# Expert products of a routed feed-forward layer: each 128-row matmul issued as two 64-row tiles with their own PSUM banks

## The chip, the cores and the metric

The kernel runs on one core of a Trainium2 chip. What is measured is the device time of one execution in microseconds (us). TensorE (PE in the profile; its weight loads are PEld) multiplies, VectorE (DVE) and ScalarE (ACT) work on tiles in SBUF and PSUM, GpSimd (POOL) issues the gathers and scatters by index, SyncE (SP) issues most other transfers. PSUM has 8 banks; a bank holds 512 float32 per partition.

## The reference, cut to what matters

```python
def conv(x, w, b):                       # depthwise, causal: 8 taps per channel
    return conv_general_dilated(x, w, (1,), padding=[(7, 0)], feature_group_count=1024) + b

def ffn(y, w_router, w_experts):         # top-1 routing over 8 experts
    idx = argmax(einsum('bsh,eh->bse', y, w_router), -1)
    all_out = einsum('bsh,efh->bsef', y, w_experts)
    return take_along_axis(all_out, idx[:, :, None, None], axis=2)[:, :, 0, :]

out = x + ffn(conv(x, cond), w_router, w_experts)   # x: 8 x 512 x 1024, experts: 8 x 1024 x 1024, float32
```

## The kernel before

There are 4096 tokens of 1024 channels. The kernel has two stages.

Stage one is the convolution. It is done on TensorE as matmuls of 128 columns (line 807, `conv`), 512 of them in four groups of two batches; each float32 matmul appears in the trace as two. ScalarE copies the results out of six PSUM banks (0 to 5, lines 435 and 436, semaphore `conv_out`). VectorE picks each token's expert (`choose`), TensorE counts places with a few bfloat16 matmuls (`rank`, banks 6 and 7), VectorE turns the places into row numbers (`place_rows`, semaphore `pos_ready`), and GpSimd scatters the convolved rows to DRAM, sorted by expert.

Stage two is the expert product. The sorted rows are taken in slots of 128 tokens of one expert: 35 slots with these inputs. For slot t:

- VectorE turns the loaded block so that channels lie on partitions (`turn_blocks`, line 683, into `y_cols`); ScalarE rounds it to the one-pass float32 type (`high_y`, line 449, `ys` HI) and VectorE subtracts to get the rest (`low_y`, line 688, `ys` LO, semaphore `ys_lo`).
- The expert's weights lie in SBUF split in the same way (`w_sb` HI and LO; ScalarE line 444, VectorE line 674 in `low_w`, semaphore `w_split`). They are replaced chunk by chunk, only when the expert changes.
- TensorE's `gemm(t, k, nth)` (line 836) makes 8 chunks of 128 channels x 3 products (HI·HI, HI·LO, LO·HI) x 2 halves of 512 output columns: 48 matmuls, all from line 851. The slot's sums lie in one of two pairs of banks, `out_banks = [4, 0]`, that is banks 4, 5 for even slots and 0, 1 for odd ones. In the last chunk the three products of the left half come first (semaphore `half_out`), then those of the right half (`gemm_chunk`).
- VectorE's `residual(t)` adds each half of the sums to the gathered row of x (lines 696 and 698); GpSimd then scatters the row to the output (line 930) and, when that has landed, gathers the x row of slot t + 2 into the same buffer (line 923).

The order of the work on each engine is written out by hand. On VectorE the loop body for slot t is `turn_blocks(t + 1)`, `residual(t - 1)`, `low_y(t + 1)`, `low_w(t + 1)`, so `low_y(t + 1)`, for which `gemm(t + 1)` waits, stands behind `residual(t - 1)`. `gemm(t)` waits for `ys_lo`, for `res_done` of slot t - 2 (its banks), and every second chunk for `w_split`. Inside `gemm(0)`, behind its third chunk, stands the last group's `rank`. Slots 0 to 2 stand ahead of a loop, the rest are in it, two to a round.

Of the kernel before, what the change touches and what calls it, by code (L numbers as in the profile page):

```python
# [6 lines left out]
ALU = mybir.AluOpType  # L7
# [9 lines left out]
BATCH, SEQ, H, TAPS, EXPERTS = 8, 512, 1024, 8, 8  # L17
TOKENS = BATCH * SEQ
HC = H // P
GROUP = 2  # L20
GROUPS = BATCH // GROUP
GT = GROUP * SEQ
TPG = GT // P
TILES = TOKENS // P
HALF = 512
# [4 lines left out]
HI, LO = 0, 1  # L30
# [10 lines left out]
SIDE = PHASES * CH  # L41
# [7 lines left out]
BANKS = -(-SETS // PER_BANK)  # L49
# [5 lines left out]
def bank_sets(n):  # L55
    return range(n * PER_BANK, min((n + 1) * PER_BANK, SETS))
# [17 lines left out]
LAST = GROUPS - 1  # L74
# [90 lines left out]
def build(nc, x_both, x_t, x_rows, factors_t, experts, consts, out):  # L165
    ctx = ExitStack()
    with ctx:  # L167
        def sb(name, shape, dt=F32):
            return ctx.enter_context(nc.sbuf_tensor(name, shape, dt))

        def over(name, shape, at, dt=F32):
            return nc.alloc_sbuf_tensor_at(name, shape, dt, offset=at)

        def sem(name):
            return ctx.enter_context(nc.semaphore(name))
# [5 lines left out]
        w_sb = sb("w_sb", [P, HC, 2, H], F32R)  # L181
# [15 lines left out]
        x_row = over("x_row", [P, RING, H], raw_at + 24 * KB)  # L197
        cmp = over("cmp", [P, 3, SLOTS, EXPERTS], x_at)
        assert 32 * KB <= row_bytes
        ys = [over("ys0", [P, 2, HC, P], raw_at, F32R), over("ys1", [P, 2, HC, P], x_at + 8 * KB, F32R)]  # L200
# [28 lines left out]
            return cst[:, at:at + n]  # L229

        ps = ctx.enter_context(nc.psum_tensor("ps", [P, 8, HALF], F32))
        out_banks = [4, 0]
        out_ps = [ps[:, b:b + 2, :].rearrange("p a n -> p (a n)") for b in out_banks]

        def conv_bank(n):
            return ps[:, n % CONV_BANKS, :]

        def rank_ps(g):
            return ps[:, 6 + g % 2, 0:(TPG + 1) * EXPERTS].rearrange("p (t e) -> p t e", t=TPG + 1)

        const_in = sem("const_in")
        factors_in = [sem(f"factors_in{k}") for k in range(len(FACTOR_PACKS))]
# [9 lines left out]
        conv_out = sem("conv_out")  # L252
# [5 lines left out]
        pos_ready = sem("pos_ready")  # L258
# [15 lines left out]
        ys_lo = sem("ys_lo")  # L274
        gemm_chunk = sem("gemm_chunk")
        half_out = sem("half_out")
        res_done = sem("res_done")
        row_out = [sem(f"row_out{k}") for k in range(RING)]

# [215 lines left out]
        def _(dve):  # L495
            V = nc.vector
# [69 lines left out]
            count, lead, others, rest, start, n_of, flag, more, nth, tmp, tail, done, sign = (per[:, i, :] for i in range(1, 14))  # L566
# [124 lines left out]

            def residual(t, k, nth_of_ring):

                dve.wait_ge(half_out, t + 1)
                dve.wait_ge(x_got[k], nth_of_ring * 16)  # L695
                V.tensor_tensor(x_row[:, k, 0:HALF], out_ps[k][:, 0:HALF], x_row[:, k, 0:HALF], ALU.add)  # L696
                dve.wait_ge(gemm_chunk, (t + 1) * HC)
                V.tensor_tensor(x_row[:, k, HALF:], out_ps[k][:, HALF:], x_row[:, k, HALF:], ALU.add).then_inc(res_done, 1)  # L698

            def low_w(t):  # L700
                new = dve.value_load(tab_i[0:1, 2, bass.ds(t, 1)], min_val=0, max_val=2)  # L701
# [17 lines left out]
            for g in range(1, GROUPS):  # L719
                n = g * PACKS  # L720
# [40 lines left out]
            slot_starts()  # L761
            low_y(2, 0)
            residual(0, 0, 1)
            slot_table()
            turn_blocks(FIRST, FIRST % RING, FIRST // RING + 1)
# [6 lines left out]
            with dve.Fori(0, ROUNDS) as i:  # L772
                with dve.If(i < last + 1):
                    for k in range(RING):
                        t = i * RING + (FIRST + k)
# [8 lines left out]
        @block.tensor  # L784
        def _(pe):
            def conv(g, s):
                n, b = g * PACKS + s // PACK, s // PER_BANK
                if s % PACK == 0:
                    if n == 0:
                        pe.wait_ge(mats_ready, 1)  # L790
                        pe.wait_ge(x_start, 16)
                    elif g == 0:
                        pe.wait_ge(mats_ready, n + 2)
                        pe.wait_ge(x_in[n % X_RING], (n // X_RING + 1) * 16)
                    else:
                        pe.wait_ge(doubled, n - PACKS + 1)
                if g == 0 and s == START_SETS:
                    pe.wait_ge(mats_ready, 2)
                    pe.wait_ge(x_in[0], 16)
                sets = bank_sets(b)  # L800
                bank = g * BANKS + b
                if s == sets[0] and bank >= CONV_BANKS:

                    pe.wait_ge(conv_out, bank - CONV_BANKS + 1)
                k = s - sets[0]
                to = conv_bank(bank).rearrange("p (u n) -> p u n", n=SIDE)[:, k:PER_BANK + 1:PER_BANK - k, :]
                mm = nc.tensor.matmul(to, xs[:, n % X_RING, s % PACK, :], mats[:, s, :].rearrange("p (u n) -> p u n", n=SIDE),  # L807
                                      start=(s == sets[0]), stop=(s == sets[-1]), skip_group_check=True)
                if s + 1 in ENDS:
                    mm.then_inc(conv_mm, 1)  # L810

            def rank(g):

                pe.wait_ge(chosen_ready, g + 1)
                pe.wait_ge(const_in, 16)
                if g >= 2:

                    pe.wait_ge(pos_ready, g - 1)
                nc.tensor.matmul(rank_ps(g)[:, 0:TPG, :], before[:, 0:P], chosen[:, :, :], start=True, stop=False,
                                 skip_group_check=True)  # L820
                for t in range(TPG):
                    mm = nc.tensor.matmul(rank_ps(g)[:, t + 1:, :], before[:, P:],
                                          chosen[:, t, :].unsqueeze(1).to_broadcast([P, TPG - t, EXPERTS]),
                                          start=False, stop=(t == TPG - 1), skip_group_check=True)
                mm.then_inc(ranked, 1)

            pe.wait_ge(warm_zero, 1)
            for n in range(START_MATMULS):
                nc.tensor.matmul(ps[:, 7, 0:P], zeros[:, :], zeros[:, :], start=True, stop=True, skip_group_check=True)
            for g in range(GROUPS):  # L830
                for s in range(SETS):
                    if g and s == 3 * PACK:
                        rank(g - 1)
                    conv(g, s)

            def gemm(t, k, nth):

                pe.wait_ge(ys_lo, t + 1)
                if not (isinstance(t, int) and t < RING):

                    pe.wait_ge(res_done, t - 1)
                for c in range(HC):
                    if nth is None:

                        pe.wait_ge(w_split, c + 1)
                    elif c % 2 == 0 and nth is not True:

                        pe.wait_ge(w_split, nth * HC + (c + 2))

                    def product(a, b, f):  # L850
                        return nc.tensor.matmul(out_ps[k][:, f * HALF:(f + 1) * HALF], ys[k][:, a, c, :],  # L851
                                                w_sb[:, c, b, f * HALF:(f + 1) * HALF],
                                                start=(c == 0 and (a, b) == (HI, HI)),
                                                stop=(c == HC - 1 and (a, b) == (LO, HI)))

                    if c < HC - 1:
                        for a, b in PRODUCTS:
                            for f in range(2):
                                mm = product(a, b, f)
                    else:  # L860
                        for a, b in PRODUCTS:
                            mm = product(a, b, 0)
                        mm.then_inc(half_out, 1)
                        for a, b in PRODUCTS:
                            mm = product(a, b, 1)
                    mm.then_inc(gemm_chunk, 1)
                    if nth is None and c == 2:
                        rank(LAST)

            def load_of(t):  # L870
                return pe.value_load(tab_i[0:1, 1, bass.ds(t, 1)], min_val=0, max_val=EXPERTS - 1)

            pe.wait_ge(conv_out, GROUPS * BANKS - 4)
            gemm(0, 0, None)
            pe.wait_ge(conv_out, GROUPS * BANKS)
            gemm(1, 1, True)
            gemm(2, 0, True)
            pe.wait_ge(table_ready, 1)
            last = pe.value_load(one_i[0:1, 3:4], min_val=0, max_val=ROUNDS - 1)
            full = pe.value_load(one_i[0:1, 5:6], min_val=0, max_val=ROUNDS)  # L880
            with pe.Fori(0, ROUNDS) as i:
                with pe.If(i < last + 1):
                    gemm(i * RING + FIRST, FIRST % RING, load_of(i * RING + FIRST))
                    with pe.If(i < full):
                        gemm(i * RING + (FIRST + 1), (FIRST + 1) % RING, load_of(i * RING + (FIRST + 1)))
# [133 lines left out]
```

## Time and profile before

| | |
|---|---|
| time, median of 2 runs | 522.23 us (520.93 and 523.53) |
| the profiled execution: its own time | 518.85 us |
| the profiled execution: span, first to last instruction | 517.0 us |
| PE busy | 503.7 us, 97% of the span |
| PEld busy | 435.7 us, 84% |
| DVE busy | 287.8 us, 56% |
| ACT busy, POOL busy | 150.5 us, 134.0 us |
| matmuls of line 851 | 1680, which is 35 slots x 48 |

A row of the profile names line, engine, operation and tile (written tile first, then the read ones), shapes, a count, busy time and the mean duration of one. The matmuls overlap in their pipeline, so their mean duration (389 ns for line 851) is longer than the time from one to the next; that time is read from a count in a stretch. Times in a timeline are from the start of the span.

### The profile page before, as it was taken

To read this page: it belongs to the slowest core of one execution; us is meant where nothing else is said; L and a number is where in the kernel's file an instruction comes from. 1 tells how busy PE (TensorE), PEld (TensorE's weight loads), DVE (VectorE), ACT (ScalarE), POOL (GpSimd) and SP (SyncE) were. 2 spreads that over 40 slices of the span, in tenths; PEclk is the share of its full clock that TensorE was granted. 3 is DMA by queue.
4 is the path that set the end of the run, shared out by engine and by line. 5 is a ranking of instruction groups with operands and counts; after the bars stand their busy time and mean duration, and the time that the engine had idled before them with its cause. 6 is when DMAs were issued, how large, how long until landed. Compare 5 with 4: busy or idle time off the path is not lost.

```text
span 517.0 us, 9479 instructions
## 1 busy us (share of the span) xinstructions
PE 503.7 (97%) x2764; PEld 435.7 (84%) x2765; DVE 287.8 (56%) x418; ACT 150.5 (29%) x255; POOL 134.0 (26%) x148
## 2 busy tenths in 40 slices
PE   8999999998997999999999999999999999999995
PEld 8999999997886877888888888888888888888884
DVE  5947373769965034499773432664347244482961
ACT  2444444376001010166530100521034011340710
POOL 0003224170650112332322321213212222222312
PEclk9999999999999999999999999999999999999999
DMA  8976999997579998689999565496658855535445
GB/s 294 411 207 211 406 283 403 335 357 262 191 301 278 318 411 219 203 275 356 377 346 305 167 196 169 134 373 188 179 180 316 255 147 151 170 105 158 130 146 171
DMA packets 59623, 130.31 MB, mean 252 GB/s; under 512 B 12752, under 2 KB 32720, under 8 KB 59600
## 3 DMA queue, kind: packets, MB, share of 16 engines
q1 hardware_dynamic: 41696, 70.12, 43.7%
q0 software_dynamic: 14832, 54.27, 29.3%
q10 hardware_dynamic: 3072, 5.65, 3.4%
q8 instruction: 10, 0.16, 0.1%
q14 instruction: 13, 0.11, 0.1%
HBM read 94.56 MB, written 35.45 MB: 251 GB/s over the span
## 4 chain that ended last, share of the span: by engine, by line
PE 63%; issue 2%; DMA 2%; DVE 0%; DVEq 0%; POOL 0%; POOLq 0%
PE ps L851 63%; DMA x_row<-x_rows,idx 2%; DVE ys L688 0%; DMA out<-x_row,idx 0%; POOL out L930 0%; DVEq L167 0%; DVEq L701 0%; DVE x_row L698 0%; POOL idx L937 0%; DVE x_row L696 0%; DVEq L703 0%; POOLq L971 0%; DVEq L695 0%; POOLq L929 0%; POOLq L922 0%
## 5 line engine op out<-in xcount | busy, mean ns | idle before, releaser
L851 PE MATMUL ps<-w_sb,ys 128*128 128x512 f32 x1680 | 382.2, 389 | 4.2 <-DVE ys L688 3.7
L851 PEld LDWEIGHTS ps<-w_sb,ys 128*128 128x128 f32 x1680 | 314.9, 188 | 70.9 <-issue 5.1
L683 DVE STREAM_TRANSPOSE y_cols<-y_blk 128x1024 f32<-128x1024 f32 x36 | 44.8, 1244 | 147.8 <-PE ps L851 122.7
L807 PE MATMUL ps<-mats,xs 128*128 128x128 f32 x1024 | 118.3, 279 | 1.2 <-DMA xs<-x_both 1.2
L807 PEld LDWEIGHTS ps<-mats,xs 128*128 128x128 f32 x1024 | 117.3, 195 | 1.7 <-DVE mats L506 1.4
L449 ACT CAST ys<-y_cols 128x1024 fp32r<-128x1024 f32 x36 | 37.9, 1053 | 275.5 <-DVE y_cols L683 267.1
L674 DVE TENSOR_TENSOR w_sb<-w_raw,w_sb 128x1024 fp32r<-128x1024 f32 x56 | 64.2, 1220 | 3.3 <-ACT w_sb L444 3.3
L930 POOL DMA_INDIRECT out<-x_row,idx x35 | 41.1, 1175 | 83.9 <-DVE x_row L698 79.9
L937 POOL COPY idx<-ids_all 128x1 int32 (+1 forms) x36 | 15.0, 416 | 178.2 <-DMA out<-x_row,idx 115.8
L444 ACT CAST w_sb<-w_raw 128x1024 fp32r<-128x1024 f32 x56 | 56.5, 1052 | 9.4 <-PE ps L851 8.3
L918 POOL DMA_INDIRECT y_sorted<-rows,pos_i x32 | 37.0, 1157 | 75.3 <-PE ps L807 55.8
L514 DVE COPY xs<-xs 56x1008 f32<-56x1008 f32 x48 | 33.2, 691 | 24.6 <-DMA xs<-x_t 22.7
L923 POOL DMA_INDIRECT x_row<-x_rows,idx x36 | 38.5, 1070 | 31.0 <-POOL idx L937 30.1
L688 DVE TENSOR_TENSOR ys<-y_cols,ys 128x1024 fp32r<-128x1024 f32 x36 | 44.0, 1223 | 0.5 <-ACT ys L449 0.5
L435 ACT COPY part<-ps 128x64 f32<-128x64 f32 x76 | 22.0, 289 | 66.6 <-PE ps L807 54.0
L436 ACT COPY rows<-ps 128x448 f32<-128x448 f32 (+1 forms) x76 | 40.8, 540 | 0.0
L696 DVE TENSOR_TENSOR x_row<-ps,x_row 128x512 f32<-128x512 f32 x35 | 23.2, 664 | 26.4 <-DMA x_row<-x_rows,idx 19.6
L698 DVE TENSOR_TENSOR x_row<-ps,x_row 128x512 f32<-128x512 f32 x35 | 23.7, 676 | 0.0
L504 DVE TENSOR_TENSOR mats<-factors 128x512 f32<-128x512 f32 (+1 forms) x17 | 11.2, 658 | 5.4 <-DMA factors<-factors_t 5.4
L506 DVE TENSOR_TENSOR mats<-factors 128x512 f32<-128x512 f32 (+1 forms) x17 | 11.2, 656 | 0.0
L674 DVE TENSOR_TENSOR w_sb<-w_first,w_sb 128x1024 fp32r<-128x1024 f32 x8 | 9.7, 1222 | 1.0 <-ACT w_sb L444 0.9
L444 ACT CAST w_sb<-w_first 128x1024 fp32r<-128x1024 f32 x8 | 8.5, 1066 | 0.0
(102 smaller groups left out, 47.1 us busy)
## 6 DMA issues: line engine op xcount, KB each, us to landing
w_raw<-experts SPq DMA_DIRECT2D x56, 512.0 KB, 8.2
y_blk<-y_sorted SPq DMA_DIRECT2D x152, 128.0 KB
xs<-x_both SPq DMA_DIRECT2D x15, 512.0 KB
xs<-x_t SPq DMA_DIRECT2D x28, 256.0 KB
xs<-x_t ACTq DMA_DIRECT2D x20, 256.0 KB
w_first<-experts SPq DMA_DIRECT2D x8, 512.0 KB, 10.2
ids_all<-y_sorted SPq DMA_DIRECT2D x38, 1.0 KB
x_row<-x_rows,idx POOLq DMA_INDIRECT x36
```

Of the source, the lines that this page charges most:

```text
L436: nc.scalar.copy(to, conv_bank(n)[:, 0:m * SIDE].rearrange("p (c j i) -> p j c i", j=PHASES, i=CH)).then_inc(conv_out, 1)
L444: nc.scalar.copy(w_sb[:, c, HI, :], raw[:, c, :]).then_inc(w_hi, 1)
L449: nc.scalar.copy(ys[k][:, HI, :, :].rearrange("p c s -> p (c s)"), y_cols[k][:, :, :].rearrange("p c s -> p (c s)")).then_inc(ys_hi, 1)
L514: V.tensor_copy(xs[old:old + USED, s, :, :].rearrange("p c (b t) -> p (c b) t", b=GROUP)[:, :, 1:], xs[new:new + USED, s, :, :].rearrange( ...
L674: V.tensor_tensor(w_sb[:, c, LO, :], raw[:, c, :], w_sb[:, c, HI, :].bitcast(F32), ALU.subtract).then_inc(w_split, 1)
L683: V.transpose(y_cols[k][:, :, :].rearrange("p m (t i) -> p t m i", t=4), y_blk[k][:, :, :, :]).then_inc(y_blocks, 1)
L688: V.tensor_tensor(ys[k][:, LO, :, :].rearrange("p c s -> p (c s)"), y_cols[k][:, :, :].rearrange("p c s -> p (c s)"), ys[k][:, HI, :, :].r ...
L807: mm = nc.tensor.matmul(to, xs[:, n % X_RING, s % PACK, :], mats[:, s, :].rearrange("p (u n) -> p u n", n=SIDE), start=(s == sets[0]), sto ...
L851: return nc.tensor.matmul(out_ps[k][:, f * HALF:(f + 1) * HALF], ys[k][:, a, c, :], w_sb[:, c, b, f * HALF:(f + 1) * HALF], start=(c == 0 ...
L918: G.indirect_dma_start(y_sorted, at(pos_i[:, g, j:j + 1]), rows[g % 2][:, j, :], None, bounds_check=last_row, oob_is_err=False).then_inc(y ...
L923: G.indirect_dma_start(x_row[:, k, :], None, x_rows, at(index), bounds_check=last_token, oob_is_err=False).then_inc(x_got[k], 16)
L930: G.indirect_dma_start(out, at(index), x_row[:, k, :], None, bounds_check=last_token, oob_is_err=False).then_inc(row_out[k], 16)
```

## The change

Each of the 48 matmuls of a slot has 128 rows (input channels) of weights and data. The change issues it as two matmuls of 64 rows, rows 0 to 63 and rows 64 to 127, each in its own row tile of TensorE's array (`tile_position` (0, 0) and (64, 0); `SIDE` is 64). Each row tile sums into its own pair of banks: banks 4, 5 and 6, 7 for even slots, 0, 1 and 2, 3 for odd ones. VectorE adds both sums to the row of x: four adds where there were two, with a semaphore `res_part` between the two that write the same half. Because a slot now holds four banks, the last group's `rank` moves to bank 0, waits there until all convolution banks are copied out, and `gemm(1)`, which writes bank 0, waits for `place_rows` of the last group.

```diff
-        out_banks = [4, 0]
-        out_ps = [ps[:, b:b + 2, :].rearrange("p a n -> p (a n)") for b in out_banks]
+        out_banks = [(4, 6), (0, 2)]
+        out_ps = [[ps[:, b:b + 2, :].rearrange("p a n -> p (a n)") for b in banks] for banks in out_banks]
...
-            return ps[:, 6 + g % 2, 0:(TPG + 1) * EXPERTS].rearrange("p (t e) -> p t e", t=TPG + 1)
+            return ps[:, 6 + g % 2 if g < LAST else 0, 0:(TPG + 1) * EXPERTS].rearrange("p (t e) -> p t e", t=TPG + 1)
...
+                left, right = slice(0, HALF), slice(HALF, H)
                 dve.wait_ge(half_out, t + 1)
                 dve.wait_ge(x_got[k], nth_of_ring * 16)
-                V.tensor_tensor(x_row[:, k, 0:HALF], out_ps[k][:, 0:HALF], x_row[:, k, 0:HALF], ALU.add)
+                V.tensor_tensor(x_row[:, k, left], out_ps[k][0][:, left], x_row[:, k, left], ALU.add).then_inc(res_part, 1)
+                dve.wait_ge(res_part, 2 * t + 1)
+                V.tensor_tensor(x_row[:, k, left], out_ps[k][1][:, left], x_row[:, k, left], ALU.add)
                 dve.wait_ge(gemm_chunk, (t + 1) * HC)
-                V.tensor_tensor(x_row[:, k, HALF:], out_ps[k][:, HALF:], x_row[:, k, HALF:], ALU.add).then_inc(res_done, 1)
+                V.tensor_tensor(x_row[:, k, right], out_ps[k][0][:, right], x_row[:, k, right], ALU.add).then_inc(res_part, 1)
+                dve.wait_ge(res_part, 2 * t + 2)
+                V.tensor_tensor(x_row[:, k, right], out_ps[k][1][:, right], x_row[:, k, right], ALU.add).then_inc(res_done, 1)
...
-                if g >= 2:
+                if g == LAST:
+                    pe.wait_ge(conv_out, GROUPS * BANKS)
+                elif g >= 2:
...
-                        return nc.tensor.matmul(out_ps[k][:, f * HALF:(f + 1) * HALF], ys[k][:, a, c, :],
-                                                w_sb[:, c, b, f * HALF:(f + 1) * HALF],
-                                                start=(c == 0 and (a, b) == (HI, HI)),
-                                                stop=(c == HC - 1 and (a, b) == (LO, HI)))
+                        for s in range(2):
+                            rows_of = slice(s * SIDE, (s + 1) * SIDE)
+                            mm = nc.tensor.matmul(out_ps[k][s][:, f * HALF:(f + 1) * HALF], ys[k][rows_of, a, c, :],
+                                                  w_sb[rows_of, c, b, f * HALF:(f + 1) * HALF],
+                                                  start=(c == 0 and (a, b) == (HI, HI)),
+                                                  stop=(c == HC - 1 and (a, b) == (LO, HI)),
+                                                  tile_position=(s * SIDE, 0))
+                        return mm
...
             pe.wait_ge(conv_out, GROUPS * BANKS - 4)
+            pe.wait_ge(pos_ready, LAST)
             gemm(0, 0, None)
-            pe.wait_ge(conv_out, GROUPS * BANKS)
+            pe.wait_ge(pos_ready, GROUPS)
             gemm(1, 1, True)
```

On VectorE, in the body of the loop, one slot's work from the turned block to the rest of `ys` stands like this before (`y_cols_53` is the block's turned tile, `ys_57` the slot's split tile, ISA and REGISTER_ALU are steps of the sequencer):

```order
283 L683 STREAM_TRANSPOSE y_cols_53<-y_blk 128x4x8x32 [waits gemm_chunk]
284 L695 ISA [waits half_out]
285 L696 TENSOR_TENSOR x_row<-ps,x_row 128x512 [waits x_got0]
286 L698 TENSOR_TENSOR x_row<-ps,x_row 128x512 [waits gemm_chunk]
287 L687 REGISTER_ALU
288 L688 TENSOR_TENSOR ys_57<-y_cols_53,ys_57 128x1024 [waits ys_hi]
```

and like this with the change:

```order
287 L684 STREAM_TRANSPOSE y_cols_53<-y_blk 128x4x8x32 [waits gemm_chunk]
288 L697 ISA [waits half_out]
289 L698 TENSOR_TENSOR x_row<-ps,x_row 128x512 [waits x_got0]
290 L699 ISA
291 L700 TENSOR_TENSOR x_row<-ps,x_row 128x512 [waits res_part]
292 L702 TENSOR_TENSOR x_row<-ps,x_row 128x512 [waits gemm_chunk]
293 L703 REGISTER_ALU
294 L704 TENSOR_TENSOR x_row<-ps,x_row 128x512 [waits res_part]
295 L688 REGISTER_ALU
296 L689 TENSOR_TENSOR ys_57<-y_cols_53,ys_57 128x1024 [waits ys_hi]
```

Two adds with waits for the add just ahead of them have come between the turned block and the subtraction that gives `ys` LO; nothing else moved.

On TensorE, the slots 1 and 2 and the start of the loop stand like this with the change (`ys_58` is the split tile of odd slots, `ys_57` that of even ones):

```order
346 L861 MATMUL ps<-w_sb,ys_58 128x512 [waits ys_lo,pos_ready]
347 L861 MATMUL ps<-w_sb,ys_58 128x512 x95
348 L861 MATMUL ps<-w_sb,ys_57 128x512 [waits res_done,ys_lo]
349 L861 MATMUL ps<-w_sb,ys_57 128x512 x95
350 L892 TENSOR_LOAD one_i [waits table_ready]
```

A slot is 96 matmuls in place of 48, each still with 512 columns, and the first of slot 1 waits for `pos_ready`, where the kernel before waited for `conv_out`.

## Rows read from the trace of the kernel before

**Rows 1.** The page: busy time, and granted TensorE clock in 40 slices
```profile
PE 503.7 (97%) x2764; PEld 435.7 (84%) x2765; DVE 287.8 (56%) x418; ACT 150.5 (29%) x255; POOL 134.0 (26%) x148
PEclk9999999999999999999999999999999999999999
```

**Rows 2.** Chain that ended last, in time order: start us, us, what
```profile
184.55 11.17 PE ps L851 x48
195.72 0.15 issue
195.87 315.14 PE ps L851 x1389
```

**Rows 3.** Windows, line 851 alone: stretch, us, busy (instructions), clock, DMA, GB/s
```profile
260.00:380.00 120.00, 120.00 (x531) 99.38 (x530) 1.00 0.70 225
```

**Rows 4.** Windows, line 807 alone (convolution, 128 columns)
```profile
20.00:40.00 20.00, 20.00 (x181) 20.00 (x180) 1.00 0.81 264
40.00:60.00 20.00, 19.93 (x179) 19.76 (x178) 1.00 0.82 298
```

**Rows 5.** Groups by line: busy us, mean ns | idle before
```profile
L851 PE MATMUL ps<-w_sb,ys 128*128 128x512 f32 x1680 | 382.2, 389 | 4.2 <-DVE ys L688 3.7 <-ACT rows L436 0.4 <-issue 0.2
L851 PEld LDWEIGHTS ps<-w_sb,ys 128*128 128x128 f32 x1680 | 314.9, 188 | 70.9 <-issue 5.1 <-ACT rows L436 0.5
L807 PEld LDWEIGHTS ps<-mats,xs 128*128 128x128 f32 x1024 | 117.3, 195 | 1.7 <-DVE mats L506 1.4 <-issue 0.2
```

**Rows 6.** Timeline of DVE, choosing: start us, us, engine, line
```profile
127.91 0.23 DVE L544 TENSOR_TENSOR logits<-logits,most 128x64 f32<-128x64 f32 x1
128.17 0.22 DVE L545 TENSOR_REDUCE top<-logits 128x8 f32<-128x64 f32 x1
```

**Rows 7.** Timeline of DVE ahead of slot 3
```profile
158.85 0.65 DVE L696 TENSOR_TENSOR x_row<-ps,x_row 128x512 f32<-128x512 f32 x1
159.42 0.67 DVE L698 TENSOR_TENSOR x_row<-ps,x_row 128x512 f32<-128x512 f32 x1
160.03 1.23 DVE L688 TENSOR_TENSOR ys<-y_cols,ys 128x1024 fp32r<-128x1024 f32 x1
```

**Rows 8.** Timeline of DVE ahead of slot 5
```profile
181.90 0.69 DVE L696 TENSOR_TENSOR x_row<-ps,x_row 128x512 f32<-128x512 f32 x1 [1.64 <-DMA x_row<-x_rows,idx]
182.51 0.68 DVE L698 TENSOR_TENSOR x_row<-ps,x_row 128x512 f32<-128x512 f32 x1
183.10 1.22 DVE L688 TENSOR_TENSOR ys<-y_cols,ys 128x1024 fp32r<-128x1024 f32 x1
```

**Rows 9.** Timeline of PE from slot 0 on, [idle before <- releaser]
```profile
129.94 28.81 PE L851 MATMUL ps<-w_sb,ys 128*128 128x512 f32 x126
...
161.49 22.07 PE L851 MATMUL ps<-w_sb,ys 128*128 128x512 f32 x96 [2.75 <-DVE ys L688]
184.55 11.17 PE L851 MATMUL ps<-w_sb,ys 128*128 128x512 f32 x48 [0.99 <-DVE ys L688]
```

**Rows 10.** Timeline of DVE, placing the last group
```profile
132.59 0.17 DVE L563 CAST pos_i<-pos 128x8 int32<-128x8 f32 x1
```

**Rows 11.** Timeline of all engines at the end
```profile
499.73 11.95 PE L851 MATMUL ps<-w_sb,ys 128*128 128x512 f32 x52
511.14 0.69 DVE L696 TENSOR_TENSOR x_row<-ps,x_row 128x512 f32<-128x512 f32 x1 [6.72 <-PE ps L851]
511.75 0.68 DVE L698 TENSOR_TENSOR x_row<-ps,x_row 128x512 f32<-128x512 f32 x1
513.26 1.01 POOL L930 DMA_INDIRECT out<-x_row,idx  x1 [1.48 <-DVE x_row L698]
```

**Rows 12.** Lines 848, 884 and 851: durations min/median/max ns, first and last start us
```profile
L848 PEldq FUSED_REGOPS  x32: 42/42/47, 161.4 to 497.7; - x32
L848 PEldq ALU_OP  x96: 32/32/32, 161.7 to 504.7; - x96
L884 PEldq COMPARE_BRANCH  x16: 71/71/73, 168.5 to 496.6; - x16
L851 PE MATMUL ps<-w_sb,ys x1680: 387/389/494, 123.8 to 511.3; 128*128 128x512 f32 x187
```

More of the change, by code:

```diff
@@ L276, in build @@
         half_out = sem("half_out")
+        res_part = sem("res_part")
         res_done = sem("res_done")
```

## The prediction

> **What bounds the kernel now.** I read the page's busy times first: TensorE is busy for 503.7 of 517.0 us, and its granted clock is full (2.4 GHz) in all 40 slices [rows 1]. So the time is TensorE's, and only its pace and its few stops count. Next the chain of waits, in order of time: from 195.87 us on it is one piece of 315.14 us with 1389 matmuls of line 851, and no other engine stands in it until the last slot is done [rows 2]. The pace is 315.14 / 1389 = 0.2269 us per matmul; a window in the middle of it says 120 / 531 = 0.2260 us [rows 3], and I use 226.9 ns. At 2.4 GHz 512 columns take 512 / 2.4 = 213.3 ns, so 13.6 ns of each are something other than streaming columns: 1680 x 13.6 ns = 22.8 us in all. That is everything the change could win on the products.
>
> The stops of line 851 add up to 4.2 us, of which 3.7 us are waits for VectorE's line 688, `low_y` [rows 5]: ahead of slot 3 (2.75 us) and of slot 5 (0.99 us) [rows 9]. VectorE's share of 56% hides that these two stops hang on it.
>
> **The change: TensorE.** A product is now two loads and two matmuls, and a slot has 96 of each. The columns per matmul stay 512. If the two row tiles run at the same time, a product still takes one stream of 512 columns in each; if they don't, it takes two in turn. No row of before shows row tiles, so I bound this from both sides.
>
> - Loads. The convolution shows the closest thing to twice the loads: each of its matmuls has its own load of 128 columns of four bytes, and 179 of them pass in 20 us, which is 111.7 ns for a load with its matmul [rows 4]; the two kinds of load are alike, 188 and 195 ns in mean [rows 5]. Two of them are 223.5 ns, 3.4 ns less than a product takes now. So neither the loads nor the sequencer, which issued those pairs at that rate, should hold two tiles back, though only just.
> - Matmuls, lower end: the 13.6 ns vanish, because one tile streams while the other changes its weights: 213.3 ns per product, -22.8 us. The 111.7 ns pace gives 223.5 ns and -5.7 us.
> - Matmuls, upper end: tiles in turn, 453.8 ns per product, +381 us.
> - I take the middle: each tile's own stream keeps the 226.9 ns that a stream takes now, since nothing in a tile's stream has changed but the number of rows, and the other tile lies beside it. Change: 0.
>
> In the trace the load of the next weights lies beside the running matmul on the same 128 rows: a load with its own turn would make the pace at least 111.7 + 213.3 = 325 ns, and it is 226.9 [rows 2, 4]. The Trainium skill (TensorE: Matmul & The Clock Gate, Part 3: Packing small matmuls, The mechanism) says that a load overlaps a running matmul only where the row group differs. For a full-height stream this trace does not agree, which is why I don't count a gain from loads that could only now be hidden. The same section's table gives 3.07 times for four row tiles, 77% of the ideal; a product at 226.9 / 0.77 = 295 ns would by that estimate add 114 us. No run here shows it yet.
>
> **The change: VectorE.** `residual` goes from two adds to four. Adds that don't depend on each other start 0.57 to 0.61 us apart (158.85, 159.42, then line 688 at 160.03) and last 0.65 to 0.69 us [rows 7, 8]. One that waits for the one ahead of it starts 0.03 us behind its end: line 544 at 127.91 lasts 0.23 us, line 545 starts at 128.17 [rows 6]. So four adds occupy 0.68 + 0.6 + 0.68 + 0.6 = about 2.6 us where two took 1.2: +1.4 us per slot, 35 x 1.4 = 49 us of VectorE, which then is busy for 337 of some 520 us. In most slots this costs nothing, since TensorE works 48 x 0.2269 = 10.9 us on a slot and has no stop after 195.87 us [rows 2]. It counts in three places, where what it delays is already waited for:
>
> - Slot 3: `low_y(3)` stands behind `residual(1)` and TensorE waits for it (160.03 + 1.23 = 161.26, matmul at 161.49) [rows 7, 9]: +1.4 us.
> - Slot 5: `residual(3)` starts when the gather of its row of x lands, and `low_y(5)` ends at 184.32, the matmul starts at 184.55 [rows 8, 9]. The gather hangs, by the scatter, on `residual(1)`, so it moves by the same 1.4 us as TensorE did; the longer `residual(3)` then adds its own +1.4 us.
> - The end: the left half is free at 511.14, the right half added by 511.75 + 0.68 = 512.43, then the last scatter is issued [rows 11]. With four adds this ends 1.4 us later: +1.4 us.
>
> Together +4.2 us. If these waits lost their cover in every slot, the bound is 35 x 1.4 = 49 us; if later gathers absorb the delay, it is only the end's 1.4 us.
>
> **The change: banks, waits, sequencer.** `gemm(1)` now waits for the last `place_rows`. That ends at 132.59 + 0.17 = 132.76 us; `gemm(1)` starts 30 matmuls after 129.94, at 136.75 [rows 9, 10]: 4 us of cover, cost nothing. `rank` moved to bank 0 waits for copies that end before TensorE gets there. The sequencer runs ahead of the array: its last wait for weights (chunk 6 of the last slot) is at 504.7 us, the last matmul starts at 511.3, so chunk 6 starts at 511.3 - 11 x 0.227 = 508.8: 4.1 us or 18 matmuls ahead. From the branch of line 884 (496.6) to the first weights' wait of the next slot (497.7) it needs 1.1 us [rows 12]. With half the columns per instruction of work, 18 matmuls are 9 products, 2.0 us: still covered.
>
> **Sum.** 518.85 us (the profiled execution, 517.0 of it the span) + 0 + 4.2 = 523.05, so **523 us**. The profiled run lies 3.4 us under the median of the two runs shown, 522.23, so I read the result as about 1% slower, within the 2% that a measurement of this kernel can tell from no change.
>
> **Rivals.**
>
> 1. *The gap between matmuls vanishes* (the side of faster). 13.6 ns per product are hidden by the other tile: 523 - 22.8 = 500 us; from 218 ns per product down, it is over 2% faster. For: a row's own gap could lie under the other tile's stream. Against: loads are hidden already, and the loads' pace of 223.5 ns lies above 218.
> 2. *The gap comes twice* or the sequencer's run-ahead fails. If the 13.6 ns belong to each change of weights and the tiles share it, a product takes 240.5 ns: +22.8, 546 us. It decides from 231 ns on. If the 1.1 us of each slot's branch come to light in 32 slots: +35, 558 us. For: two loads of 111.7 ns leave only 3.4 ns, and 2.0 us of run-ahead is only twice what a branch needs.
> 3. *A tile's load waits for its own matmul.* Each tile then takes 111.7 + 226.9 = 338.6 ns per product, both tiles side by side: 523 + 1680 x 111.7 ns = 711 us. This is what the Trainium skill's rule above would give. Against: the overlap on the same rows in the trace of before. Anything halfway between one and two streams falls here too.
> 4. *The tiles don't run together.* 453.8 ns per product: 523 + 381 = 904 us. The change then does not do what it says. For: no row shows two matmuls in the array. Against: the two tiles share neither rows nor banks.
>
> **How the numbers follow.** Forecast (224 to 231 ns a product; 514 to 529 us) 0.47; rival 1, 0.15; rival 2, 0.18; rival 3, 0.08; rival 4, 0.12. Faster by over 2%: 0.15. Within 2%: 0.47. Slower: 0.18 + 0.08 + 0.12 = 0.38. The range reaches from rival 1 to the far end of rival 2, 500 to 558 us, and leaves out rivals 3 and 4, 0.20. The likeliest case alone has 514 to 529.
>
> **What would show it.** In the profile after: 3360 matmuls of line 861 with the count per stretch doubled (1062 in 120 us) for the forecast, 1130 for rival 1, near 530 for rival 4, near 710 for rival 3. The four adds should take 2.6 us from first start to `low_y`; the stops ahead of slots 3 and 5 should be about 1.4 us longer each, and the last add should end 2.7 us after its first began. A stop at each slot's first matmul with nothing that it waits for would be the sequencer. The forecast is wrong if the pace of a product leaves 224 to 231 ns; VectorE alone can't move it by 2%.

## The result, and the profile after

The changed kernel takes 531.14 us (median of 529.4 and 532.89) where the kernel before takes 522.23: a ratio of 1.0189, 95% interval 1.0128 to 1.025. Beside other kernels on a second chip it came out at 531.32 against 520.4 us, ratio 1.0168 (1.0106 to 1.023). The ratios here and below are estimates from the runs of both kernels, each with its interval; the plain quotients of the medians differ a little (1.0171 and 1.0210). So it is slower by 1 to 2.5%. The forecast was 523 us, about 1% slower, in a range of 500 to 558.

The profiled execution took 532.89 us with a span of 530.7 us, 13.7 us more than the span before. It is the longer of the two executions shown, and the profiled one of the kernel before (518.85 us) is the shortest of three, so the two traces differ by more than the medians do (8.9 us). Its page begins (busy us, share, count; then the granted clock in 40 slices):

```profile
PE 508.5 (96%) x4444; PEld 465.8 (88%) x4445; DVE 334.9 (63%) x488; ACT 150.2 (28%) x255; POOL 133.5 (25%) x148
...
PEclk9999999999899989999999899999999999999998
```

Against [rows 1]: 1680 more matmuls and loads, 47 us more of VectorE, only 4.8 us more of TensorE, and a clock that is no longer full everywhere. Line 861 alone, in a stretch without stops (stretch, us, busy and count of PE and PEld, clock):

```profile
300.00:420.00 120.00, 120.00 (x1062) 109.75 (x1061) 1.00 0.66 213
```

1062 matmuls are 531 products in 120 us, exactly the count of [rows 3]: a product of two tiles keeps the pace of one full-height matmul. So the loss lies elsewhere. The timeline of TensorE, whose last bracket is the idle time before a piece and what ended it:

```profile
131.07 0.24 PE L827 MATMUL ps<-chosen,cst 128*128 128x64 bf16 x1 [2.66 <-DVE chosen L551]
...
131.50 31.54 PE L861 MATMUL ps<-w_sb,ys 64*128 64x512 f32 x252
163.44 22.08 PE L861 MATMUL ps<-w_sb,ys 64*128 64x512 f32 x192 [0.40 <-DVE ys L689]
188.61 67.19 PE L861 MATMUL ps<-w_sb,ys 64*128 64x512 f32 x576 [3.09 <-DVE ys L689]
256.54 22.06 PE L861 MATMUL ps<-w_sb,ys 64*128 64x512 f32 x192 [0.74 <-DVE ys L689]
279.37 11.18 PE L861 MATMUL ps<-w_sb,ys 64*128 64x512 f32 x96 [0.77 <-DVE ys L689]
293.53 230.39 PE L861 MATMUL ps<-w_sb,ys 64*128 64x512 f32 x2016 [2.98 <-DVE ys L689]
```

Where [rows 9] had two stops on `low_y`, there are five, 8.0 us in sum, and three of them (256.54, 279.37, 293.53) stand where TensorE had none before [rows 2]. The first matmul after the last `rank` starts 1.56 us later than before (131.50 for 129.94), that of slot 3 1.95 us, that of slot 5 4.06 us; the last matmul starts at 523.5 for 511.3 [rows 12], 12.2 us later. Nothing shows the 1.56 us to be the change's: ahead of the last `choose` VectorE waited 1.74 us for the transfer of a block, where it had waited 0.46, and nothing that the change touches stands before that. In the variants below that do all the work the same start lies between 129.78 and 131.77 us.

What stands behind the last and longest of the new stops is in the chain of waits, in order of time (start us, us, what):

```profile
267.95 10.04 DMA out<-x_row,idx
278.28 0.92 POOL idx L950
...
280.04 9.36 DMA x_row<-x_rows,idx
289.43 0.70 DVE x_row L698
...
292.24 1.07 DVE ys L689
293.53 229.73 PE ps L861 x2007
```

A slot's row of x is gathered into the buffer from which another slot's result is scattered: the scatter (10.04 us) must land, then the index is copied, the gather (9.36 us) lands, and only then can `residual` begin, with `low_y` behind it. The expert weights load at the same time: eight loads of 512 KB are issued from 265.89 us on, and they land after 9.6 us (median).

The scatters of slots 10 and 12, which share a buffer, give the length of a round of this loop (timeline of GpSimd, here and then in the kernel before):

```profile
267.95 1.93 POOL L943 DMA_INDIRECT out<-x_row,idx  x1 [0.30 <-issue]
293.22 1.01 POOL L943 DMA_INDIRECT out<-x_row,idx  x1 [0.30 <-issue]
...
258.83 1.93 POOL L930 DMA_INDIRECT out<-x_row,idx  x1 [0.30 <-issue]
282.22 1.01 POOL L930 DMA_INDIRECT out<-x_row,idx  x1 [0.30 <-issue]
```

From one to the next are 25.3 us, 23.4 in the kernel before, and TensorE needs only 2 x 10.9 = 21.8 us for two slots. So even before the change the loop was slower than TensorE in this stretch, but TensorE did not yet have to wait there.

The second part of the loss is the clock. Windows over all engines (stretch, us, busy and count of PE, PEld, DVE, ACT, POOL, then clock, DMA, GB/s):

```profile
124.00:132.00 8.00, 5.30 (x47) 4.86 (x49) 6.02 (x12) 2.04 (x3) 0.00 (x0) 0.90 0.39 107
132.00:165.00 33.00, 32.60 (x266) 27.72 (x264) 25.82 (x70) 2.10 (x2) 15.65 (x16) 0.92 0.75 256
165.00:190.00 25.00, 21.91 (x188) 20.11 (x186) 10.68 (x13) 2.21 (x3) 3.94 (x6) 0.97 1.04 339
190.00:195.00 5.00, 5.00 (x38) 4.14 (x36) 0.00 (x0) 0.94 (x1) 0.61 (x1) 0.81 1.03 404
...
260.00:295.00 35.00, 31.26 (x272) 26.54 (x270) 24.07 (x26) 10.60 (x11) 9.43 (x9) 0.99 0.85 260
295.00:300.00 5.00, 5.00 (x36) 4.13 (x34) 3.70 (x5) 0.53 (x1) 0.83 (x2) 0.73 0.76 251
```

After three stops (2.66, 3.09 and 2.98 us) the clock stood at its lower level, 1.2 GHz, for a while. With only two levels, a mean of 0.92 over 33 us is 33 x 0.08 x 2 = 5.3 us at the lower one; the six rows together give 1.6 + 5.3 + 1.5 + 1.9 + 0.7 + 2.7 = 13.7 us. At that level a product takes nearly twice as long (427 ns, seen with one tile alone in an experiment below), so the estimate is a cost of about 13.7 x (1 - 227/427) = 6.4 us, a little less as the first fall began within the stop. The pieces agree: the 252 matmuls from 131.50 us on take 31.54 us, where a variant below with a full clock took 28.86. Part of that cost is not a loss: what the clock took between 131 and 163 us shortened the stop ahead of slot 3 from 2.75 to 0.40 us.

The end is as forecast (timeline, all engines):

```profile
523.39 0.69 DVE L698 TENSOR_TENSOR x_row<-ps,x_row 128x512 f32<-128x512 f32 x1 [5.30 <-PE ps L861]
524.12 0.69 DVE L700 TENSOR_TENSOR x_row<-ps,x_row 128x512 f32<-128x512 f32 x1
524.72 0.68 DVE L702 TENSOR_TENSOR x_row<-ps,x_row 128x512 f32<-128x512 f32 x1
525.44 0.69 DVE L704 TENSOR_TENSOR x_row<-ps,x_row 128x512 f32<-128x512 f32 x1
```

526.13 - 523.39 = 2.74 us where [rows 11] show 512.43 - 511.14 = 1.29: 1.45 us more.

### The profile page after: what moved, and what is told of

Same layout as the page of the kernel before. It is cut to its first block, busy times and chain, and to the rows that moved or that the text cites. A ratio compares the mean times of both kernels' runs of the same rounds, so it can differ in the third digit from the quotient of the medians.

```text
span 530.7 us, 12976 instructions
## 1 busy us (share of the span) xinstructions
PE 508.5 (96%) x4444; PEld 465.8 (88%) x4445; DVE 334.9 (63%) x488; ACT 150.2 (28%) x255; POOL 133.5 (25%) x148
## 4 chain that ended last, share of the span: by engine, by line
PE 50%; DMA 7%; issue 5%; DVE 4%; ACT 1%; POOL 1%; DVEq 1%; ACTq 0%; POOLq 0%
PE ps L861 50%; DMA x_row<-x_rows,idx 4%; DMA out<-x_row,idx 4%; DVE w_sb L675 1%; ACT w_sb L445 1%; DVE x_row L702 1%; DVE x_row L698 1%; DVE y_cols L684 0%; POOL idx L950 0%; DVE ys L689 0%; DVEq L707 0%; DVE x_row L704 0%; POOL out L943 0%; DVEq L710 0%; ACTq L458 0%
## 5 line engine op out<-in xcount | busy, mean ns | idle before, releaser
L861 PE MATMUL ps<-w_sb,ys 64*128 64x512 f32 x3360 | 388.8, 391 | 8.5 <-DVE ys L689 8.0
L861 PEld LDWEIGHTS ps<-w_sb,ys 64*128 64x128 f32 x3360 | 347.2, 187 | 49.5 <-issue 10.1
L813 PE MATMUL ps<-mats,xs 128*128 128x128 f32 x1024 | 116.3, 276 | 3.3 <-DMA xs<-x_both 1.6
L813 PEld LDWEIGHTS ps<-mats,xs 128*128 128x128 f32 x1024 | 115.0, 192 | 4.1 <-DVE mats L507 2.3
L950 POOL COPY idx<-ids_all 128x1 int32 (+1 forms) x36 | 16.6, 462 | 171.3 <-DMA out<-x_row,idx 142.0
L931 POOL DMA_INDIRECT y_sorted<-rows,pos_i x32 | 35.2, 1101 | 73.5 <-PE ps L813 54.1
L515 DVE COPY xs<-xs 56x1008 f32<-56x1008 f32 x48 | 33.3, 694 | 24.8 <-DMA xs<-x_t 23.4
L698 DVE TENSOR_TENSOR x_row<-ps,x_row 128x512 f32<-128x512 f32 x35 | 23.2, 663 | 30.1 <-DMA x_row<-x_rows,idx 24.8
L700 DVE TENSOR_TENSOR x_row<-ps,x_row 128x512 f32<-128x512 f32 x35 | 24.2, 691 | 1.2
L704 DVE TENSOR_TENSOR x_row<-ps,x_row 128x512 f32<-128x512 f32 x35 | 24.2, 691 | 1.2
L702 DVE TENSOR_TENSOR x_row<-ps,x_row 128x512 f32<-128x512 f32 x35 | 23.8, 680 | 0.0
```

The costliest lines, as they stand in the source:

```text
L515: V.tensor_copy(xs[old:old + USED, s, :, :].rearrange("p c (b t) -> p (c b) t", b=GROUP)[:, :, 1:], xs[new:new + USED, s, :, :].rearrange( ...
L861: mm = nc.tensor.matmul(out_ps[k][s][:, f * HALF:(f + 1) * HALF], ys[k][rows_of, a, c, :], w_sb[rows_of, c, b, f * HALF:(f + 1) * HALF], s ...
L931: G.indirect_dma_start(y_sorted, at(pos_i[:, g, j:j + 1]), rows[g % 2][:, j, :], None, bounds_check=last_row, oob_is_err=False).then_inc(y ...
```

## The experiments

The theory drawn from this profile (T): the row tiles cost and bring nothing; the loss comes from the two more adds per slot, through the chain residual, scatter, gather, residual, and from the clock that falls at the stops. Its rivals: the row tiles themselves cost (R1), it is the spread of transfers between runs (R2), VectorE's longer work delays `low_y` by itself, with no chain (R3).

### The changed kernel once more

> The changed kernel once more, beside the kernel before and the three variants on one chip. Theory (T): a product keeps its pace as two row tiles, and the whole loss comes from the two more adds per slot, by the chain residual, scatter, gather into the same buffer, residual, which makes TensorE stop for VectorE's line 689 and lets its clock fall after the longest stops: ratio 1.013 to 1.025, stops of 6 to 10 us in sum, some stretches at half clock. Rival (R1), the row tiles themselves cost: the same ratio. Rival (R2), the loss is mostly the spread of transfers between runs: a ratio within 1.01.

Measured: 531.32 us (527.14 to 531.92) against 520.4, ratio 1.0168 (1.0106 to 1.023); five stops on line 689 of 10.2 us in sum. The loss is there on another chip, with an interval that leaves out 1.01, so R2 is out as its cause.

### Full height, still four adds

```diff
-                        for s in range(2):
-                            rows_of = slice(s * SIDE, (s + 1) * SIDE)
...
+                        s = c // (HC // 2)
+                        return nc.tensor.matmul(out_ps[k][s][:, f * HALF:(f + 1) * HALF], ys[k][:, a, c, :],
+                                                w_sb[:, c, b, f * HALF:(f + 1) * HALF],
...
```

> Matmuls of the full 128 rows again, 48 a slot, but with two pairs of banks per slot (chunks 0 to 3 sum into one pair, 4 to 7 into the other), so that VectorE still makes four adds with the same waits. T: as the changed kernel, ratio to before 1.012 to 1.025 (about 528 to 535 us), with the same new stops in the loop. R1: as before, within 1.005.

Measured: 528.11 us, ratio 1.0137 (1.0088 to 1.0185). Four of its five stops (timeline of TensorE) come at the same slots as the changed kernel's on this chip, 3, 5, 6 and 11 (164.53, 189.62, 203.41 and 258.96 us there); the last is ahead of slot 13, the changed kernel's ahead of slot 14 (293.76 us):

```profile
162.51 23.68 PE L860 MATMUL ps<-w_sb,ys 128*128 128x512 f32 x96 [3.90 <-DVE ys L689]
187.59 11.15 PE L860 MATMUL ps<-w_sb,ys 128*128 128x512 f32 x48 [1.40 <-DVE ys L689]
200.20 54.82 PE L860 MATMUL ps<-w_sb,ys 128*128 128x512 f32 x240 [1.45 <-DVE ys L689]
255.74 22.05 PE L860 MATMUL ps<-w_sb,ys 128*128 128x512 f32 x96 [0.72 <-DVE ys L689]
278.93 239.64 PE L860 MATMUL ps<-w_sb,ys 128*128 128x512 f32 x1056 [1.14 <-DVE ys L689]
```

The four adds alone, without any row tile, bring most or all of the loss: 7.7 of 10.9 us by the medians (528.11 and 531.32 against 520.4), with intervals that overlap.

### Row tiles, two adds

```diff
-                V.tensor_tensor(x_row[:, k, left], out_ps[k][0][:, left], x_row[:, k, left], ALU.add).then_inc(res_part, 1)
-                dve.wait_ge(res_part, 2 * t + 1)
-                V.tensor_tensor(x_row[:, k, left], out_ps[k][1][:, left], x_row[:, k, left], ALU.add)
+                V.tensor_tensor(x_row[:, k, left], out_ps[k][0][:, left], x_row[:, k, left], ALU.add)
...
```

> The row tiles stay, 96 matmuls a slot, but VectorE adds the first tile's sum only, two adds as before; the second tile's sum is left out of the result. T: as before, ratio 0.995 to 1.005 (518 to 524 us), a product every 227 ns. R1: ratio above 1.012, as the changed kernel.

Measured: 522.79 us, ratio 1.0018 (0.9983 to 1.0053), and again 1062 matmuls in 120 us:

```profile
300.00:420.00 120.00, 120.00 (x1062) 109.76 (x1060) 1.00 0.68 220
```

The row tiles alone cost nothing that can be measured; the interval leaves room for 0.5%. R1 is out as the cause of the loss. The stop ahead of slot 3 is 3.06 us here, and there is none ahead of slots 5, 6 and 11, where four adds had them; two small ones are left, 1.42 us ahead of slot 12 for the weights and 0.92 us ahead of slot 14 for `low_y`.

### The result in a tile of its own

```diff
+        out_row = over("out_row", [P, RING, H], x_at + 16 * KB)
...
-                V.tensor_tensor(x_row[:, k, left], out_ps[k][0][:, left], x_row[:, k, left], ALU.add).then_inc(res_part, 1)
+                V.tensor_tensor(out_row[:, k, left], out_ps[k][0][:, left], x_row[:, k, left], ALU.add).then_inc(res_part, 1)
...
             scatter(0, 0, 0)
-            pool.wait_ge(row_out[0], 16)
             look_up(2, 0, 2, 3)
```

> The changed kernel with four adds, but residual writes its result to a tile of its own (out_row), so that the gather of the x row of slot t + 2 needs only residual(t) and not the landing of its scatter; a scatter still waits for the one ahead of it. T: the stops from slot 6 on vanish and the ratio falls to 1.000 to 1.010 (522 to 527 us); what remains is the 1.4 us at the end and the stops near slot 0 and 3. Rival (R3), VectorE's longer work ahead of low_y alone makes the stops: the ratio stays at 1.013 to 1.025.

The edit also gives each scatter its own copy of the index, made by GpSimd. Measured: 526.24 us, ratio 1.0092 (1.0054 to 1.0129); each of its six runs (523.69 to 526.79) lies under each of the four of the changed kernel on the same chip. TensorE's timeline from slot 0 on:

```profile
131.77 28.86 PE L866 MATMUL ps<-w_sb,ys 64*128 64x512 f32 x252
165.11 90.00 PE L866 MATMUL ps<-w_sb,ys 64*128 64x512 f32 x768 [4.47 <-DVE ys L692]
255.82 261.50 PE L866 MATMUL ps<-w_sb,ys 64*128 64x512 f32 x2304 [0.72 <-DVE ys L692]
```

With the gather freed from the landing of the scatter, the stops ahead of slots 5, 6 and 14 are gone, though VectorE does all four adds and `low_y` still stands behind them: that is the chain, and R3 doesn't explain these stops. What is left is the stop at slot 3, now 4.47 us, with a clock of 0.77 in the 12 us after it, 0.72 us ahead of slot 11, and the end. For the stop at slot 3 R3 does hold: `low_y(3)` stands behind four adds, and with two it was 3.06 us on the same chip.

### `low_y` ahead of `residual`

```diff
-                        residual(t - 1, (r + 1) % RING, i + ((FIRST + k - 1) // RING + 1))
                         low_y(t + 1, (r + 1) % RING)
+                        residual(t - 1, (r + 1) % RING, i + ((FIRST + k - 1) // RING + 1))
```

> As e6 (own tile for the result, four adds, row tiles), and low_y(t + 1) now stands ahead of residual(t - 1) on VectorE. T: the stop ahead of slot 3, which e6 still had with 4.5 us, falls to about 3 us, since low_y(3) no longer stands behind the longer residual(1); ratio 1.002 to 1.007 (521.5 to 524 us), what is left being the 1.4 us at the end. R3 (VectorE's 1.4 us more per slot cost wherever they stand): ratio stays at 1.009 or rises.

Measured: 540.45 us, ratio 1.0359 (1.0319 to 1.0399): a miss, and the slowest of the kernels that do all the work. TensorE's waits (engine, line, waited for, us in total, times, longest), and VectorE ahead of slot 3:

```profile
PE ps L866 <- DVE out_row L709: 12.9, 7, 6.8
PE ps L866 <- DVE w_sb L678: 4.4, 1, 4.4
...
162.24 1.23 DVE L692 TENSOR_TENSOR ys<-y_cols,ys 128x1024 fp32r<-128x1024 f32 x1 [1.11 <-ACT ys L453]
163.38 0.68 DVE L703 TENSOR_TENSOR out_row<-ps,x_row 128x512 f32<-128x512 f32 x1
...
165.42 0.69 DVE L709 TENSOR_TENSOR out_row<-ps,out_row 128x512 f32<-128x512 f32 x1
```

Slot t + 1 needs `residual(t - 1)` as much as `low_y(t + 1)`, since it writes the same banks; I had overlooked that. In the old order the adds fill the time in which ScalarE rounds the block (1.05 us); in the new one VectorE waits 1.1 us in nearly every slot (34 waits, 37.4 us in sum) and the adds come after, on TensorE's path.

### The own tile without the change

```diff
-                V.tensor_tensor(x_row[:, k, 0:HALF], out_ps[k][:, 0:HALF], x_row[:, k, 0:HALF], ALU.add)
+                V.tensor_tensor(out_row[:, k, 0:HALF], out_ps[k][:, 0:HALF], x_row[:, k, 0:HALF], ALU.add)
...
```

> The kernel before (full height, two adds), with the own tile for the result as in e6. T: its only stop in the loop that hangs on a gather, 0.99 us ahead of slot 5, vanishes: ratio 0.995 to 1.000 (518 to 520.5 us). R3: no change, 1.000.

Measured: 521.14 us, ratio 1.0002 (0.9973 to 1.003): no gain. In its trace the x row is no longer waited for at slot 5, but the block of slot 5 itself came late (VectorE waited 17.43 us for its transfer) and TensorE stopped for 4.38 us (timelines of VectorE and TensorE):

```profile
183.89 1.25 DVE L686 STREAM_TRANSPOSE y_cols<-y_blk 128x1024 f32<-128x1024 f32 x1 [17.43 <-DMA ids_all<-y_sorted]
...
187.70 328.11 PE L856 MATMUL ps<-w_sb,ys 128*128 128x512 f32 x1440 [4.38 <-DVE ys L691]
```

With two adds, cutting the chain gains nothing that can be measured, so the 5.1 us that the own tile brought above belong to the four adds. No version here beats the kernel before.

### One tile alone, and both on the same rows

```diff
-                        for s in range(2):
+                        for s in range(1):
```

> Only the matmuls of the first row tile, 48 of 64 rows a slot, and two adds; the second tile's products are left out. T: the second tile lies wholly beside the first, so leaving it out saves nothing: a product every 227 ns, time 518 to 524 us. Rival (R4), the two tiles partly take turns and something else got faster: less than 500 us.

Measured: 846.45 us in one run, far from both. TensorE's timeline from the last `rank` on, then windows over all engines:

```profile
129.42 0.23 PE L823 MATMUL ps<-chosen,cst 128*128 128x64 bf16 x1 [1.50 <-DVE chosen L551]
...
129.85 709.49 PE L857 MATMUL ps<-w_sb,ys 64*128 64x512 f32 x1662
...
125.00:130.00 5.00, 3.50 (x23) 2.60 (x22) 4.21 (x11) 1.05 (x1) 0.00 (x0) 0.88 0.44 106
130.00:135.00 5.00, 5.00 (x12) 3.90 (x13) 4.60 (x12) 0.00 (x0) 2.71 (x4) 0.50 0.17 29
...
300.00:420.00 120.00, 120.00 (x283) 91.99 (x282) 45.65 (x44) 26.30 (x26) 15.07 (x18) 0.50 0.53 171
```

After a stop of 1.50 us ahead of the last `rank` the clock went to 1.2 GHz and stayed there to the end, through 709 us in which TensorE never stopped: 1662 matmuls in 709.49 us, 427 ns each.

```diff
-                            rows_of = slice(s * SIDE, (s + 1) * SIDE)
+                            rows_of = slice(0, SIDE)
...
-                                                  tile_position=(s * SIDE, 0))
+                                                  tile_position=(0, 0))
```

> 96 matmuls a slot as in e2, but both of a product use rows 0 to 63 of data and array (tile position 0 for both), into the two pairs of banks; the products of rows 64 to 127 are left out and two adds are made. T: two matmuls on the same rows take turns: 454 ns per product, about 900 us. R4: the array takes two matmuls at a time whatever their rows: about 520 us.

Measured: 894.65 us in one run, with line 857 at

```profile
300.00:420.00 120.00, 120.00 (x532) 97.39 (x531) 1.00 0.57 180
```

532 matmuls in 120 us, 226 ns each, 451 ns for a product of two: on the same rows they take turns, on different rows they run side by side. Here TensorE had no stop on the way and the clock stayed full.

### One tile alone, with the stops filled

```diff
+                        fill(FILL_RANK)
                         rank(LAST)
...
             gemm(2, 0, True)
+            fill(FILL_LOOP)
```

> As e3 (the first row tile alone, two adds, the second tile's products left out), but TensorE fills the two places where e3 or the kernel before stopped, ahead of the last rank and ahead of the loop, with 24 and 48 full-height bfloat16 matmuls of 128 columns on zeros, into a bank that nothing reads. In e3 the clock fell at the stop ahead of the last rank and never rose again. If the fall hangs on a stop, the clock stays at 2.4 GHz here and a product takes 227 ns with one tile as with two: 519 to 527 us. If one tile of 64 rows can't hold the clock at all, it falls without a stop and the time is 830 to 850 us again.

Measured: 825.08 us in one run, just under the second of the two ranges. It answers both questions, at different times (timeline of TensorE, then windows with line 863 alone):

```profile
130.44 28.86 PE L863 MATMUL ps<-w_sb,ys 64*128 64x512 f32 x126
159.23 2.85 PE L844 MATMUL ps<-zeros 128*128 128x128 bf16 x48
163.90 654.04 PE L863 MATMUL ps<-w_sb,ys 64*128 64x512 f32 x1536 [1.82 <-issue]
...
131.00:157.00 26.00, 26.00 (x116) 21.10 (x115) 1.00 0.68 246
300.00:420.00 120.00, 120.00 (x282) 93.12 (x282) 0.50 0.45 141
```

Without a stop the clock held through slots 0 to 2: 126 matmuls of one tile in 28.86 us, and the changed kernel with own tile needs the same 28.86 us for 252 of two tiles. The second tile is free. Then a stop of 1.82 us, for which the trace names no cause, was left ahead of slot 3; the clock fell and did not come back in 654 us. So one tile kept a full clock that it had, and did not regain one that was lost; with both tiles the clock came back within microseconds each time. Why the one and not the other was not tested further.

## Why the prediction was right, and where it was not

**The pace.** Right: 0 us per product was predicted and 1062 matmuls in 120 us named as its sign; that is the count. Rivals 1, 2 (its first form), 3 and 4 are out by the same row: the gap of 13.6 ns neither vanished nor doubled, loads did not wait for matmuls, tiles did not take turns. The lower bound that I took from hidden gaps had no ground: the gap is there in one tile's stream alone (28.86 us / 126 = 229 ns, the last matmul's tail included) and in two side by side. The rule of the Trainium skill weighed there (TensorE: Matmul & The Clock Gate, Part 3, The mechanism: the list there says that loads overlap only with matmuls of another row group) does not hold in the variant on the same rows either, where each load is on the rows of the running matmul and the pace is still 226 ns. The text above that list also lets a load into a background weight buffer run ahead, which no run here tells apart. What the Trainium skill says in the same Part 3 of tiles, that they run their matmuls concurrently, this trace agrees with: 226 ns for the two. The estimate of 295 ns from its table of speedups does not fit: 226 ns.

One reading of the prediction was wrong beside this: 111.7 ns is the time of a load with its matmul, not of a load alone, so the 325 ns for loads in turn, and the 338.6 ns of rival 3, were too high. No run shows what a load alone would cost; the conclusion stands by the pace on the same rows, 226 ns, which leaves 12 to 13 ns beside the 213.3 ns of the columns.

**The sequencer, banks and new waits.** Right: no stop names `pos_ready` or `place_rows`, and the stretch from 293.53 us on has none for 230.39 us, though twice the instructions are issued.

**VectorE.** The duration was right: four adds at 160.06 - 159.37 = 0.69, 0.60, 0.72 and 0.61 us from one to the next, 2.62 us for the four, and 47 us more busy time for 49 foretold. The end was right: 1.45 us for 1.4. The sign named for slots 3 and 5, stops longer by 1.4 us each, did not come: they were 0.40 us for 2.75 and 3.09 for 0.99, and 3.96 and 1.44 on the second chip. The wrong step is the one that said "In most slots this costs nothing, since TensorE works 48 x 0.2269 = 10.9 us on a slot and has no stop after 195.87 us". It took TensorE's freedom from stops for room. The room that counted was that of a loop through two transfers, and it was thin. Two rows of the waits before say so, and I did not weigh them (engine, line, waited for, total us, times, longest):

```profile
POOL idx L937 <- DMA out<-x_row,idx: 115.8, 25, 10.2
DVE x_row L696 <- DMA x_row<-x_rows,idx: 19.6, 7, 7.7
```

GpSimd waited for a landing before most of its gathers, and VectorE for a gather in seven slots. While weights load, a scatter lands after some 10 us and a gather after some 9 (267.95 and 280.04 above); with the copies between, `residual` itself and the other slot's transfers in the same queue that is more than the 21.8 us of two slots (25.3 us above), so that 1.4 us more in each `residual` comes out at TensorE again and again, not once. I had that bound (49 us if the cover were lost everywhere) and the three places (4.2 us); the term came out between. The whole difference is by the medians 531.14 - 522.23 = 8.9 us on the first chip and 10.9 on the second; the four adds alone brought 7.7 there, 1.4 of it the end. The own tile for the result, which cuts this loop, took 5.1 us of it away (531.32 to 526.24).

**The clock.** It had no term. I read a full clock in every slice of one execution and took it as given; after three stops of the changed kernel it fell, about 6 us of its profiled run. The kernel before does not always keep it either: on the second chip its fifteen executions have mean granted clocks of 0.989 to 0.998. Their mean is 0.994, that of the changed kernel's four executions 0.990. By the working above that is about 6 and 11 us at the lower level, so some 2 us of the 10.9 are the clock's; this is an estimate, since these means take in idle time too.

**The sum.** It starts from the profiled execution, 518.85 us, the shortest of the three shown; from the median, 522.23 us, the same terms give 526.4, and the measured 531.14 us lies 4.7 us above that. It lies outside the 514 to 529 us of the likeliest case, though the pace was that case's. The stated range holds it only because it reached on to 558 us for rival 2, whose causes, a second gap and a sequencer that falls behind, did not occur: in that the range was luck.

So the sign, the mechanism of the pace and the time within 2% were forecast; VectorE's term was sized at 4.2 us, about half of the 7.7 us that four adds alone brought.

## What to carry to other kernels

- Two 64-row tiles side by side brought as much as one matmul of 128 rows here, no more: splitting a full contraction in tiles bought nothing on the array and was paid for in PSUM banks and in one more add for each half.
- An engine's spare time says nothing about a step that stands in a loop through transfers. Follow the buffer round: what frees it, what fills it, who waits for that, and compare the sum with the time of a round.
- Moving a step off one wait can put another on the path: before reordering, list every semaphore for which the bottleneck waits, not only the one that came last.

## What was not expected of the hardware

- Stops of 2.66 to 3.09 us in the changed kernel were followed by stretches at 1.2 GHz, while the profiled execution of the kernel before, with one of 2.75 us [rows 9], kept a full clock behind it [rows 1]. The length alone does not decide it in these runs.
- A stream of one 64-row tile, without a stop, held 2.4 GHz for 29 us when it had it, and stayed at 1.2 GHz for 654 and 709 us after a stop of 1.82 and 1.50 us. Two tiles side by side came back each time. With one tile the kernel thus took about 60% longer (825 and 846 us against 521 and 522) with the same count of matmuls. Half of the rows alone does not bring the clock down: the variant with both on the same rows had no stop and held 2.4 GHz for 754 us. Whether it would have regained a lost clock was not tested.
